# Row maxima of self-attention from 64-row products, both key halves of a tile side by side in the array

## What is computed

```
x = x + attention(layer_norm(x), layer_norm(x))      # self: 16 heads of 64, 1024 keys
x = x + attention(layer_norm(x), ctx)                # cross: 77 context rows
x = x + geglu_feed_forward(layer_norm(x))            # inner width 1024
attention: softmax(q @ k.T / 8) @ v, then @ wo + bo
```

## Time and profile before

| | |
|---|---|
| median of 3 runs | 2130.04 us (2129.46 to 2131.5) |
| the profiled execution, its own time | 2130.59 us |
| its span, first to last instruction | 2128.9 us |
| mean granted TensorE clock | 0.996 of full speed |
| busy share of the span: PE, DVE, ACT, POOL | 98%, 75%, 69%, 65% |
| matmuls of the maxima (line 1028) | 1024, of 512 columns |
| reductions of the maxima (line 1628) | 1024, 684 ns each |

### The profile page before, as it was taken

The page is one execution under the profiler, slowest core; times in us unless marked ns, Lnnn a source line. Parts: engine busy times, 40 slices in busy tenths (PEclk is TensorE's granted clock), DMA queues, the critical chain, the costliest instruction groups (busy, mean ns, idle before and its releaser), DMA issues.

```text
span 2128.9 us, 58916 instructions
## 1 busy us (share of the span) xinstructions
PE 2075.7 (98%) x25120; PEld 1414.2 (66%) x25120; DVE 1595.6 (75%) x3014; ACT 1474.5 (69%) x1950; POOL 1382.1 (65%) x896
## 2 busy tenths in 40 slices
PE   6999999999999999999999999999999999999999
PEld 2666666685666666678566666667856666667675
DVE  6888887557688888765768888866577888886654
ACT  4888889345488888934558888883465888887442
POOL 6878886464378887745347888784434888776532
PEclk8999999999999999999999999999999999999999
DMA  4322220050332232004032233110503323210120
GB/s 136 81 56 66 67 67 23 21 106 18 81 90 66 57 78 62 27 14 103 26 95 76 66 79 78 39 36 7 100 18 95 86 64 83 67 39 22 29 58 21
DMA packets 132581, 127.82 MB, mean 60 GB/s; under 512 B 81760, under 2 KB 94048, under 8 KB 132320
## 3 DMA queue, kind: packets, MB, share of 16 engines
q1 hardware_dynamic: 132080, 123.66, 23.2%
q10 hardware_dynamic: 240, 0.39, 0.1%
HBM read 55.72 MB, written 4.19 MB: 28 GB/s over the span
## 4 chain that ended last, share of the span: by engine, by line
PE 87%; DVE 6%; POOL 2%; ACT 2%; issue 2%; DMA 1%; SPq 0%; POOLq 0%; DVEq 0%
PE work L1028 10%; PE scores L1052 9%; PE scores L1045 9%; PE scores L937 8%; PE scores L939 8%; PE scores L938 8%; PE work L1074 5%; PE work L1070 5%; PE work L1072 5%; PE work L937 4%; PE work L939 4%; PE work L938 4%; POOL prob L873 2%; DVE minima L1628 1%; DVE prob L1639 1%
## 5 line engine op out<-in xcount | busy, mean ns | idle before, releaser
L873 POOL TENSOR_TENSOR prob<-prob 128x1024 f16<-128x1024 f32 x328 | 711.5, 2185 | 288.7 <-ACT prob L1427 272.3
L1628 DVE TENSOR_REDUCE minima<-work 128x1 f32<-128x512 f32 x1024 | 682.8, 684 | 53.5 <-PE work L1028 47.4
L1426 ACT ACTIVATE prob<-scores 128x1024 f32<-128x1024 f32 x512 | 528.3, 1032 | 86.1 <-PE scores L1052 67.8
L1427 ACT ACTIVATE prob<-scores 128x1024 f16<-128x1024 f32 x512 | 525.3, 1026 | 0.0
L1070 PE MATMUL work<-vals,prob 128*128 128x65 f16 x4096 | 429.4, 192 | 11.5 <-POOL prob L873 10.2
L1070 PEld LDWEIGHTS work<-vals,prob 128*128 128x128 f16 x4096 | 383.1, 99 | 77.3 <-issue 22.2
L1074 PE MATMUL work<-vals,prob 128*128 128x65 f16 x4096 | 430.0, 195 | 0.0
L1072 PE MATMUL work<-vals,prob 128*128 128x64 f16 x4096 | 429.8, 193 | 0.0
L1072 PEld LDWEIGHTS work<-vals,prob 128*128 128x128 f16 x4096 | 380.1, 97 | 52.4
L1028 PE MATMUL work<-ka,qa 128*128 128x512 f16 x1024 | 391.3, 384 | 21.4 <-DVE minima L1628 15.4
L1074 PEld LDWEIGHTS work<-vals,prob 128*128 128x128 f16 x4096 | 380.5, 97 | 0.0
(11 more groups left out here) (174 smaller groups left out, 4150.3 us busy)
## 6 DMA issues: line engine op xcount, KB each, us to landing
qa<-staged_q SPq DMA_DIRECT2D x128, 128.0 KB, 2.3
ka<-staged_k SPq DMA_DIRECT2D x126, 128.0 KB, 2.3
raw_even<-in_pairs SPq DMA_DIRECT2D x32, 384.0 KB, 3.3
raw_odd<-in_pairs SPq DMA_DIRECT2D x32, 384.0 KB, 3.4
raw_odd<-in_pieces SPq DMA_DIRECT2D x20, 512.0 KB, 3.3
raw_even<-in_pieces SPq DMA_DIRECT2D x20, 512.0 KB, 3.2
qb<-staged_q SPq DMA_DIRECT2D x64, 128.0 KB, 2.3
kb<-staged_k SPq DMA_DIRECT2D x63, 128.0 KB, 2.3
```

The costliest lines, as they stand in the source:

```text
L873: pool.tensor_tensor(prob[1][:, slot, :], prob32[:, slot, :], prob[0][:, slot, :], ALU.subtract).then_inc(a.polished, 1)
L1426: act.activation(prob32[:, n % RING, :], source, ACT.Exp)
L1427: act.activation(prob[0][:, n % RING, :], source, ACT.Exp)\
L1628: dve.tensor_reduce(minima[:, t, h:h + 1], out[:, :], AX.X, ALU.max, negate=True)\
```

## The change

The products of the maxima leave out the lower part of the keys: a tile's first key half comes from `qa` and `ka` on the 64 partitions "mine", its second from `qa` on the 64 partitions "others" (where the upper part of the queries lies too) and a new tile `km` on these partitions, which holds the upper part of keys 512 to 1023. The two are issued one after the other, to the two PSUM banks, in the two row halves of the array. `km` lies in `xn`, the buffer of the normalised rows, which is free then, one quarter of it for each parity of the pair; one DMA more per head fills it. PE waits for both reductions of the tile before, once, and both products stand at the start of the step; DVE's two reductions so stand ahead of the step's `take`. The second tile of a step, where there is one, stands at the step's end. Since the shift is used alike over a whole row, the softmax is the same for any of them.

```
-MOVES = 12
+MOVES = 14
...
-        out += [step for step in peaks_of[s] if step.kind == "arrive"] + peaks[:1]
-        spread = [peaks[1:2], peaks[2:3], peaks[3:]] if len(peaks) > 2 else [[], peaks[1:], []]
+        out += [step for step in peaks_of[s] if step.kind == "arrive"] + peaks[:2]
+        spread = [[], [], peaks[2:]]
...
+        km = [xn[:, p, :].bitcast(F16) for p in range(2)]
...
-            return [(ka_[mine, :], up), (ka_[others, :], low), (kb_[mine, :], up)]
+            return [(ka_[mine, :], up), (km[par][others, :], up[:, BLK:2 * BLK]), (ka_[others, :], low),
+                    (kb_[mine, :], up)]
...
-                        out = next_peak()
                         t, h = s
+                        if h:
+                            return
+                        n = pace.here(*PEAK)
+                        mine, others = [slice(r, r + DH) for r in (head * DH, (1 - head) * DH)]
...
-                        pe.matmul(out[:, :], qa[par][head][:, first_query:first_query + (P - 1) * HALF + 1:HALF],
-                                  ka[par][head][:, h * BLK:(h + 1) * BLK], start=True, stop=True)\
-                            .then_inc(a.peak_full, 1)
+                        pe.wait_ge(a.peak_free, pace.n(*PEAK) + 2)
+                        pe.matmul(self_peaks[n % PEAK_RING][:, :], qa[par][head][mine, queries_],
+                                  ka[par][head][mine, 0:BLK], start=True, stop=True).then_inc(a.peak_full, 1)
+                        pe.matmul(self_peaks[(n + 1) % PEAK_RING][:, :], qa[par][head][others, queries_],
+                                  km[par][others, :], start=True, stop=True).then_inc(a.peak_full, 1)
```

More of the change, by code:

```diff
@@ L960, in bank @@
                     return high_bank(n)
-                def next_peak():
-                    pe.wait_ge(a.peak_free, pace.n(*PEAK) + 1)
-                    return self_peaks[pace.here(*PEAK) % PEAK_RING]
                 def weight(kind, c, column):
@@ L1024, in do @@
                             pe.wait_ge(a.head1_ready, pace.n("arrive", times=8 * MOVES) + CREDIT)
-                        out = next_peak()
                         t, h = s
+                        if h:
+                            return
+                        n = pace.here(*PEAK)
+                        mine, others = [slice(r, r + DH) for r in (head * DH, (1 - head) * DH)]
                         first_query = t // HALF * BLK + t % HALF
-                        pe.matmul(out[:, :], qa[par][head][:, first_query:first_query + (P - 1) * HALF + 1:HALF],
-                                  ka[par][head][:, h * BLK:(h + 1) * BLK], start=True, stop=True)\
-                            .then_inc(a.peak_full, 1)
+                        queries_ = slice(first_query, first_query + (P - 1) * HALF + 1, HALF)
+                        pe.wait_ge(a.peak_free, pace.n(*PEAK) + 2)
[3 more added lines that the diff above has]
+                                  km[par][others, :], start=True, stop=True).then_inc(a.peak_full, 1)
                     elif step.kind == "score":
```

## The result

The changed kernel takes 2180.75 us (median of 4 runs, 2176.0 to 2182.78) against 2130.32 of the kernel before (4 runs): a ratio of 1.0233, 95% interval 1.0221 to 1.0246, so 50 us slower. The execution profiled took 2182.78 us, with a span of 2181.0 and a mean granted clock of 0.991 (0.996 before).

What follows compares the result with a forecast made beforehand. PE was taken to bound the kernel, a row of matmuls without a hole. Tile 12, wait for both reductions 4, two-tile steps 12 and rest 8 gave +36 us: 2166 us, 1.7% slower; 8-in-10 range 2085 to 2195.

Steps and rivals of the forecast that it cites:

- the tile: Two 64-row products of each of 512 tiles on PE: 0.455 us against 0.432, 0.023 more each, +12 us.
- The two gaps: PE's changes from 128 rows to 64 and back: 0.09 us each, taken from transposes using 8 columns amid 124-column scores.
- the load on the way in: Weights of a tile's first 64-row product, loaded in the open: 0.025 us over the 0.215 of streaming.
- the stagger: Start of a tile's second product behind its first: between 0 and 0.03 us, taken as 0.015.
- The way out: From the 64-row pair back to 128 rows: a gap of 0.09 us plus 0.02 for the load.
- free change of rows: Rival: array passes between 128 and 64 rows without the gap, a tile saves 0.2 us; 2092 us, chance 0.18.
- The wait for both reductions: PE waits for both reductions of the tile before: 0.15 us in each of 32 pairs of heads, +4 us.
- the account of head 1: Step 3 of head 1: reductions end 0.66 us too late, the refine starts 0.60 earlier, so 0.05 stays.
- The take that I counted at nothing: DVE's take, one reduction later, awaited by the next placed block: nothing counted, since ACT has it ready only after the scores.
- Two-tile steps: Three steps of each round's first unit, second tile at the end: 1.43 us wait each, +12 us (4 to 18).
- The rest: First tiles ahead of self-attention 3.6 us, tiles beside the last projections 2, keys' DMA 2: +8 us together (3 to 14).
- the DMA of keys: One DMA more for head 0's keys delays its last by 0.60 us, hidden by 0.4 there; 2 us for all pairs.

## Why the prediction was right, and where its sizes were off

The direction was right, and so was the kind of cost, a change of rows that eats up what the halves save, and waits for DVE. The range held: 2166 was forecast, 2181 measured. That the forecast came so near is in part luck. Of its 36 us 12 stood on the tile, which cost nothing; the 24 that it had for waits, order and DMAs are half of the 50 measured. By the starts of the score products in the two traces (the first of each step, before against after), the growth lies ahead of self-attention (4.3 us, forecast 3.6), in the first units (15.1, forecast 12), in the stages between the rounds' self-attentions (3.3, forecast 2) and in the other units: 29.5, where the forecast had 18 with the tile and 6 without it. PE's idle time ahead of the maxima that DVE ended was to rise to about 35 us, most of it in first units. It rose to 43.7: 17.4 in first units, 16.7 in the other units, 8.4 ahead of self-attention and 1.3 beside the projections.

The runs make a ladder of four parts, each the difference of two medians:

| from, to | us | forecast |
|---|---|---|
| before (2130.9) to changed order, two waits, 128 rows (2155.1) | +24.2 | with the next row 4 + 12 + 3.6 + 2 = 22 |
| to one wait (2173.8) | +18.7 | |
| to the additional DMAs (2181.2) | +7.4 | 2 |
| to 64 rows, side by side (2180.75) | -0.4 | +12 |

The order of the ladder matters, as the two-wait runs show (18.7 with 128 rows, 5 with 64); the sum doesn't. A part is good to some 3 us, as far as runs of one kernel differ.

**The tile: +12 forecast, about 0 measured.** The two gaps are there, as taken from a change of columns. The sum for a tile held 0.455; the trace gives 0.43. Two small terms were too large: the load on the way in, 0.025, lies within the 0.09; the stagger is 0.00 in the timeline (3 to 4 ns over the 512 pairs), not 0.015. The way out, 0.12 with the load in it, was put at 0.11. The Trainium skill, "TensorE: Matmul & The Clock Gate", section "Measured speedup vs the span model", has row-packed products start some 4 ns apart; the trace agrees. That alone would have given the *free change of rows*, which was wrong by the whole price of the change: 0.217 us, against the 0.215 that the halves give back.

**The wait for both reductions: +4 forecast, more measured.** With 128 rows the one wait costs 14 us in the units behind the first (29.7 with it, 15.4 without). The step that failed is the account of head 1. I let the refine of step 2 start 0.60 earlier, since a reduction no longer stood ahead of it. The timeline of the changed kernel there:

```profile
208.43 1.28 DVE L1632 TENSOR_REDUCE minima<-work 128x1 f32<-128x512 f32 x2
210.22 0.69 DVE L1597 SCALAR_TENSOR_TENSOR vals<-work,vals 128x512 f16<-128x512 f32 x1 [0.51 <-ACT vals L1396]
210.83 1.22 DVE L1643 TENSOR_TENSOR prob<-prob 128x1024 f16<-128x1024 f32 x1
...
211.96 1.28 DVE L1632 TENSOR_REDUCE minima<-work 128x1 f32<-128x512 f32 x2
...
213.30 0.40 PE L1031 MATMUL work<-ka,qa 64*128 64x512 f16 x1
```

What stands ahead of the refine now is the `take`, and that waits 0.51 for ACT. The reductions end at 213.24 and PE goes at 213.30, some 0.2 later than it could, where 0.05 was forecast; 24 such places make 4.6 us. It is the wait that the run with one more `polish` removed, for 5.5 us.

**The take that I counted at nothing.** "ACT has it ready only after the scores" was right for the values and wrong for `merge`, whose four transposes ahead of the scores ACT empties at once. In the changed kernel:

```profile
129.44 0.61 ACT L1401 ACTIVATE oT<-work 128x512 f16<-128x512 f32 x1
...
129.63 1.28 DVE L1632 TENSOR_REDUCE minima<-work 128x1 f32<-128x512 f32 x2
...
130.83 0.68 DVE L1603 TENSOR_TENSOR oT<-work,oT 128x512 f16<-128x512 f32 x1
...
131.56 0.27 PE L939 MATMUL work<-wpC,cT 128*124 128x128 f16 x1 [0.19 <-DVE oT L1603]
```

ACT is done at 130.05, while DVE is at the two reductions; the `take` follows both, and the next placed block waits. From the pair to this block are 0.59 us, not 0.34: in the trace 20 blocks behind a `merge` start so late, by 0.26 each, 5 us. Before, this `take` stood between the two reductions, and the block started without a wait named:

```profile
119.21 0.68 DVE L1599 TENSOR_TENSOR oT<-work,oT 128x512 f16<-128x512 f32 x1
...
119.96 0.26 PE L937 MATMUL work<-wpC,cT 128*124 128x128 f16 x1
```

**Two-tile steps: +12 forecast, +12 measured.** By the starts of the score products the three steps grow by 2.9 us in each of the rounds 2 to 4, near the 3.3 worked out (by 5.3 in the first, with the lower clock). A place waits 1.58, near the 1.43 worked out:

```profile
589.26 0.38 PE L1031 MATMUL work<-ka,qa 64*128 64x512 f16 x1 [1.58 <-DVE minima L1632]
```

The reason given, one wait for both reductions, is the smaller part of it: with 128 rows the three steps still grow by 2.4 a round where each product waits for its own reduction, against 3.1 with the one wait. It is the new place of the second tile that costs.

**The rest: +8 forecast.** The first tiles come 2.00 us apart, as forecast. Two things were missed. The clock, which I left out: PE, idle for most of the first tiles, is granted the full level 14 us later, and 7 us come back when it is kept busy. And the DMA of keys, 7.4 for 2. SP's queue in one pair:

```profile
199.32 0.60 SPq L665 DMA_DIRECT2D kb<-staged_k  x1
...
203.22 0.40 PE L1031 MATMUL work<-ka,qa 64*128 64x512 f16 x1 [1.24 <-DMA kb<-staged_k]
```

The delay is the 0.60 of an issue, as forecast, but PE has the keys only 3.9 us behind the issue's start (199.32 to 203.22), where I took the median of 2.3. Why this one takes longer stays open; 12 of the 64 key DMAs of this kind took over 3 us in the kernel before too.

Of the order's 24 us, 7.9 lie in the first units and 7.6 in the late blocks behind `merge`; the rest was not taken apart.

## What to carry to other kernels

Packing products into row halves pays only for what runs between one change of rows and the next: here two products of 512 columns save 0.215 us and the change there and back, with the weight load that it lays open, takes 0.217. Price a change of the used array from any such place in the trace, both ways, before counting on the halves. And when two products are bound together, their wait, their reductions and their order on the other engine are bound too: that, not the array, cost the 50 us, and it could be seen by running the new order with the old products. Taking the bond off again, with a wait for each product, helped the old products (18.7 us) far more than the halves (5 us), of which 89 pairs in 512 then no longer start together.

## What was not expected of the hardware

The way out of the row halves took 0.12 us after both halves had worked and 0.095 after one alone; the way in was the same 0.09. Sixty-four-row products of the two halves started within 3 to 4 ns of each other whenever neither had to wait. And a stall of PE in the first 14 us of work lasted into the next 16, through the granted clock.
